# The last attention window's output product ahead of the expert tiles, and VectorE's routing cut into other pieces

## The reference

```
x: [2, 2048, 256], 16 heads of 16
scores  = 0 everywhere, q.k/4 inside each window of 128, plus q.k/4 among 64 global tokens
attn    = softmax(scores over all 2048 keys) @ v        # keys outside the window count with score 0
x1      = layernorm(x + attn @ wo.T + bo)
expert  = argmax(x1 @ Wg.T) over 8 experts
xhat    = layernorm(x1)
h       = gelu((xhat * ln_scale[e] + ln_bias[e]) @ W1[e] + b1[e])      # 64 wide
y       = h @ W2[e] + b2[e]                                            # e = expert of the token
out     = layernorm(x1 + y)
```

## Time and profile before

| what | us |
|---|---|
| runs of the kernel (3) | 398.56, 399.14, 401.33; median 399.14 |
| the profiled execution | 401.99 |
| its span, first to last instruction | 400.2 |
| busy in the span: PE, DVE, ACT, POOL | 342.2, 284.2, 226.9, 201.5 |

### The profile page before, as it was taken

How to read it: one execution, slowest core, us unless ns; L and a number is a source line. 1 busy time by engine, 2 the same in 40 slices (tenths; PEclk the granted TensorE clock), 3 DMA queues, 4 the chain that set the end, 5 groups by cost and what they waited for, 6 DMA issues and landing times.

```text
span 400.2 us, 12415 instructions
## 1 busy us (share of the span) xinstructions
PE 342.2 (85%) x4438; PEld 284.0 (71%) x4438; DVE 284.2 (71%) x829; ACT 226.9 (57%) x521; POOL 201.5 (50%) x352
## 2 busy tenths in 40 slices
PE   4989899999999999999989999988775798999400
PEld 3858688887887888887868888776453786877300
DVE  7795547676567675777888778796968796788810
ACT  3325476655665566556658866656653444777620
POOL 5243133443553435434447877844854343376772
PEclk9999999999999999999999999999999688999855
DMA  8762662100000000001013212100113554563220
GB/s 236 227 208 70 207 199 85 28 2 26 26 1 26 7 20 26 4 28 28 2 29 70 85 51 91 43 16 2 72 44 100 152 198 127 152 206 107 87 83 0
DMA packets 27981, 31.74 MB, mean 79 GB/s; under 512 B 5183, under 2 KB 25882, under 8 KB 27931
## 3 DMA queue, kind: packets, MB, share of 16 engines
q1 hardware_dynamic: 20246, 18.22, 15.9%
q0 software_dynamic: 3456, 8.66, 5.9%
q10 hardware_dynamic: 4230, 4.22, 3.2%
HBM read 20.96 MB, written 11.17 MB: 80 GB/s over the span
## 4 chain that ended last, share of the span: by engine, by line
PE 54%; DVE 24%; issue 7%; ACT 7%; POOL 3%; DMA 2%; SPq 0%; POOLq 0%; DVEq 0%; ACTq 0%
DVE row_max_t L1186 13%; PE ps L1436 8%; PE ps L1473 8%; PE ps L1398 7%; PE ps L1428 6%; PE ps L1703 5%; PE ps L1456 4%; PE ps L1721 3%; ACT probs L896 3%; PE ps L1450 3%; POOL out_dram L719 2%; PE ps L1420 2%; PE ps L1689 2%; PE ps L1440 2%; ACT boundsT_t L907 2%
## 5 line engine op out<-in xcount | busy, mean ns | idle before, releaser
L896 ACT ACTIVATE probs<-ps 128x1024 f32<-128x1024 f32 x64 | 62.1, 1022 | 59.9 <-PE ps L1440 59.7
L1186 DVE TENSOR_REDUCE row_max_t<-ps 128x16 f32<-128x2048 f32 x31 | 70.9, 2286 | 21.5 <-PE ps L1428 21.4
L1436 PE MATMUL ps<-q_slots,k_slots 32*128 32x256 f32 x512 | 40.5, 400 | 10.2 <-DVE row_max_t L1186 9.1
L663 POOL TENSOR_TENSOR attn_t<-num_t,rden_t 128x256 f32<-128x256 f32 x32 | 19.9, 621 | 54.1 <-DVE rden_t L1215 54.0
L746 ACT ACTIVATE pvT_t<-ps 128x512 f32<-128x512 f32 x34 | 20.3, 598 | 38.6 <-PE ps L1450 35.8
L646 POOL TENSOR_TENSOR bounds_t<-guard_t,bounds_t 128x16 f32<-128x16 f32 x32 | 7.1, 222 | 68.8 <-DVE guard_t L1197 68.7
L1428 PE MATMUL ps<-k_slots,q_slots 32*128 32x128 f32 x1056 | 38.7, 283 | 3.0 <-DVE dg L1037 1.3
L1428 PEld LDWEIGHTS ps<-k_slots,q_slots 32*128 32x128 f32 x1056 | 32.5, 186 | 8.9 <-issue 6.0
L719 POOL DMA_INDIRECT out_dram<-other_tiles x32 | 31.5, 985 | 11.7 <-issue 7.0
L907 ACT ACTIVATE boundsT_t<-ps,head_mask 128x128 fp32r<-128x128 f32 x128 | 36.7, 381 | 0.9 <-PE ps L1619 0.7
L620 POOL DMA_INDIRECT sorted_rows<-rows,place_i x32 | 31.7, 990 | 10.1 <-issue 6.3
(11 more groups left out here) (278 smaller groups left out, 796.9 us busy)
## 6 DMA issues: line engine op xcount, KB each, us to landing
table<-rest_sums SPq DMA_DIRECT2D x4, 1088.0 KB, 6.1
other_tiles<-sorted_rows SPq DMA_DIRECT2D x32, 136.0 KB, 2.4
xs<-in_L_attn_x_dram SPq DMA_DIRECT2D x16, 256.0 KB, 2.7
rows<-in_L_attn_x_dram ACTq DMA_DIRECT2D x4, 1024.0 KB, 7.4
sorted_rows<-pad_rows SPq DMA_DIRECT2D x9, 136.0 KB, 1.8
first_tiles<-sorted_rows SPq DMA_DIRECT2D x8, 136.0 KB, 2.1
w<-in_L_ffn_W_dram SPq DMA_DIRECT2D x2, 256.0 KB, 8.2
w<-in_L_ffn_W_dram SPq DMA_DIRECT2D x1, 512.0 KB
```

What stands on the lines that cost most here:

```text
L896: act.activation(probs[:, 2 * h:2 * h + 2, :], ps[:, 2 * h:2 * h + 2, :], ACT.Exp).then_inc(probs_ready, 1)
L1186: dve.tensor_reduce(row_max[:], ps_all, op=ALU.max, axis=AX.X).then_inc(max_ready, 1)
L1436: mm(ps[:, u, 2 * c * P:(2 * c + 2) * P], k_slots[quad(u), s, c, :], q_slots[quad(u), s, c, :, :].rearrange("p a n -> p (a n)"), start=Tru ...
```

## The change

It sets `PAIRS_FROM` to 34, so pair 0 comes at the end of step 34, behind the output product of window 31; pair 1 follows the ranks of the last batch in step 35. `turn_tiles(0)` and the registers of pair 0 move to the end of step 33. In `pair_steps` the registers of pair i+1 are read behind the first layer of pair i, except at pair 8, where the second list begins.

`route` is cut in two: `choose` takes its last three operations and, for the first batch, runs within step 19. The ranks of that batch come in step 20, its places in step 20, its factors in four pieces in steps 21 to 23. ACT's scalings start in step 24 and POOL's scatters in step 25, the last ones of the first two batches in step 31. The scalings of the third batch move from step 35 to 34, those of the fourth from pair 3 to pair 2.

The groups of results become seven: (0,2), (2,4), (4,8), (8,12), (12,16), (16,18), (18,20) in pairs. `list_tiles(1)` comes after `finish(1)` and the first `normalise` in place of after `finish(0)`.

```diff
--- before.py
+++ after.py
@@ -449,12 +449,12 @@
         LOOP_A = (4, 16)
         AHEAD = 2
         WEIGHTS_AT = 22
-        RANKS_AT = (19, 27, 33, 35)
-        PAIRS_FROM = NW + 1
-        SCALED_AT = {22: (0, 5), 23: (5, 10), 24: (10, 16), 29: (16, 20), 30: (20, 24), 35: (24, 30)}
-        SCATTERED_AT = {23: (0, 2, 3), 24: (3, 5, 6), 25: (6, 8, 9), 26: (9, 11, 12), 27: (12, 14, 15), 28: (15, 16, 16),
-                        30: (16, 19, 20), 31: (20, 22, 23), 32: (23, 24, 24)}
-        FACTORS_DONE = {22: 1, 29: 2, 35: 3}
+        RANKS_AT = (20, 27, 33, 35)
+        PAIRS_FROM = NW + 2
+        SCALED_AT = {24: (0, 5), 25: (5, 10), 26: (10, 16), 29: (16, 20), 30: (20, 24), 34: (24, 30)}
+        SCATTERED_AT = {25: (0, 2, 3), 26: (3, 5, 6), 27: (6, 8, 9), 28: (9, 11, 12), 29: (12, 14, 15), 30: (15, 18, 19),
+                        31: (19, 22, 24)}
+        FACTORS_DONE = {24: 1, 29: 2, 34: 3}
 
         def attention_steps(eng, step, first, split=None, between=None):
             for t in range(first, LOOP_A[0]):
@@ -473,7 +473,7 @@
 
 
 
-        GROUPS = ((0, 2), (2, 6), (6, 10), (10, 14), (14, 18), (18, 20))
+        GROUPS = ((0, 2), (2, 4), (4, 8), (8, 12), (12, 16), (16, 18), (18, 20))
 
         def final_places():
 
@@ -840,7 +840,7 @@
                     keep_tiles(i + 1)
                 for g, t in FINALS[i]:
                     final(g, t)
-                if i == 3:
+                if i == 2:
                     act.wait_ge(ln_ready, NB)
                     act.wait_ge(centred, NW)
                     for w in range(*BATCHES[-1]):
@@ -863,8 +863,10 @@
                 if not steady and t == 3:
                     act.wait_ge(out_gate_in_psum, 1)
                     copy(out_biasT[:].rearrange("p c n -> p (c n)"), ps_rao[:, HID:2 * HID]).then_inc(out_biasT_ready, 1)
-                if not steady and t > PAIRS_FROM:
-                    pair_steps(t - PAIRS_FROM - 1)
+                if not steady and t == PAIRS_FROM:
+                    keep_tiles(0)
+                if not steady and t >= PAIRS_FROM:
+                    pair_steps(t - PAIRS_FROM)
                 if not steady and t == 0:
                     act.wait_ge(xsum_in_psum, 1)
                     copy(pvT[:], ps_rao).then_inc(xsum_ready, 1)
@@ -881,8 +883,6 @@
                     act.activation(e_val[:, 1 - p, :], e_arg[:, 1 - p, :], ACT.Exp).then_inc(e_ready, 1)
                 if live(t + 1, steady) and p:
                     values_of(t + 1, (s + 1) % SLOTS, False)
-                if not steady and t == PAIRS_FROM:
-                    keep_tiles(0)
                 if not steady and t in SCALED_AT:
                     if t in FACTORS_DONE:
                         act.wait_ge(ln_ready, FACTORS_DONE[t])
@@ -912,7 +912,7 @@
 
             attention_steps(act, step, first=0)
 
-            for i in range(NW + 3 - PAIRS_FROM, PAIRS):
+            for i in range(NW + 4 - PAIRS_FROM, PAIRS):
                 pair_steps(i)
             keep_hidden(PAIRS - 1)
             for g, t in LAST_FINALS:
@@ -1099,6 +1099,13 @@
                 link(dve.tensor_tensor(zc[:, part, :], z_all[:, part, :], gate_bias[:].unsqueeze(1).broadcast_to(per_expert), ALU.add))
                 link(dve.tensor_reduce(zmax[:, 0, part], zc[:, part, :], op=ALU.max, axis=AX.X))
                 link(dve.tensor_tensor(hit[:, part, :], zc[:, part, :], zmax[:, 0, part].unsqueeze(2).broadcast_to(per_expert), ALU.is_equal))
+
+            def choose(b):
+
+                first, end = BATCHES[b]
+                n = end - first
+                part = slice(first, end)
+                per_expert = [P, n, EXPERTS]
                 link(dve.tensor_tensor(hit[:, part, :], hit[:, part, :], rank[:].unsqueeze(1).broadcast_to(per_expert), ALU.mult))
                 link(dve.tensor_reduce(zmax[:, 1, part], hit[:, part, :], op=ALU.max, axis=AX.X))
                 dve.tensor_tensor(onehot[:, part, :], hit[:, part, :], zmax[:, 1, part].unsqueeze(2).broadcast_to(per_expert),
@@ -1249,12 +1256,14 @@
 
                 if t == 17:
                     late_constants()
+                if t == 19:
+                    choose(0)
                 if t == 21:
-                    factors(0, 9, FACTOR_STEPS)
+                    factors(0, 0, 4)
                 if t == 23:
+                    factors(0, 10, FACTOR_STEPS)
+                if t == 25:
                     select_parts()
-                if t == 25:
-                    hidden_constants()
                 if t == 28:
                     factors(1, 4, 8)
                 if t == 30:
@@ -1263,16 +1272,21 @@
 
             def between_steps(t):
 
+                if t == 16:
+                    hidden_constants()
                 if t == 18:
                     route(0)
-                if t == 19:
+                if t == 20:
                     find_places(0)
-                if t == 20:
-                    factors(0, 0, 9)
-                if t in (21, 22):
-                    scale_first_layer(t - 21)
+                if t == 21:
+                    factors(0, 4, 6)
+                if t == 22:
+                    factors(0, 6, 10)
+                if t in (24, 25):
+                    scale_first_layer(t - 24)
                 if t == 26:
                     route(1)
+                    choose(1)
                 if t == 27:
                     find_places(1)
                     factors(1, 0, 4)
@@ -1286,6 +1300,7 @@
                     fold_first_bias()
                 if t == 32:
                     route(2)
+                    choose(2)
                     mark_tiles(0)
                     stack_first_bias()
                 if t == 33:
@@ -1293,6 +1308,7 @@
                     factors(2, 0, FACTOR_STEPS)
                 if t == 34:
                     route(3)
+                    choose(3)
                 if t == 35:
                     take_ranks(3)
                     dve.wait_ge(ranks_taken, NB)
@@ -1381,11 +1397,11 @@
             attention_steps(dve, step, first=0)
             for i in range(PAIRS):
                 finish(i)
-                if i == 0:
-                    list_tiles(1)
                 for g, (a, b) in enumerate(GROUPS):
                     if b == i + 1:
                         normalise(g)
+                if i == 1:
+                    list_tiles(1)
 
 
         @block.tensor
@@ -1552,8 +1568,6 @@
                     pe.wait_ge(v_ready, t - 1)
                     pe.wait_ge(boundsT_ready, upto(t))
                     weigh(va[:, (s + 2) % SLOTS, 0:HEADS * VP], probs).then_inc(pv_in_psum, 1)
-                if not steady and t == PAIRS_FROM:
-                    turn_tiles(0)
                 if not steady and t == 0:
                     sum_windows()
                 if not steady and t == 0:
@@ -1636,6 +1650,10 @@
                 if not steady and t == RANKS_AT[-1]:
                     pe.wait_ge(residual_ready, NW)
                     ranks(NB - 1)
+                if not steady and t == PAIRS_FROM - 1:
+                    turn_tiles(0)
+                    pe.wait_ge(lists_ready, 1)
+                    held[0] = experts_of(0)
                 if not steady and t >= PAIRS_FROM:
                     pair_steps(t - PAIRS_FROM)
 
@@ -1727,10 +1745,12 @@
                 if i == 0:
                     pe.wait_ge(experts_ready, 1)
                     pe.wait_ge(ld_w2, 32)
-                if 2 * i in (0, TILES[0]):
-                    pe.wait_ge(lists_ready, 1 + (i > 0))
-                held[i] = experts_of(i)
+                if 2 * i == TILES[0]:
+                    pe.wait_ge(lists_ready, 2)
+                    held[i] = experts_of(i)
                 first_layer(i, held[i])
+                if i + 1 < PAIRS and 2 * (i + 1) != TILES[0]:
+                    held[i + 1] = experts_of(i + 1)
                 if i > 0:
                     turn_hidden(i - 1)
                 if i + 1 < PAIRS:
```

## The result

The changed kernel is slower: median 410.25 us (410.14 to 410.98, 4 runs) against 399.98 (398.56 to 401.33, 4 runs of the kernel before). The ratio is 1.0261, with a 95% interval of 1.0218 to 1.0304, so about 10 us. 395.0 was forecast, in a range of 392.0 to 398.9.

What follows compares the result with a forecast made beforehand. DVE's reduction in the attention steps, PE's idle and low-clock seam, and POOL's scatters at the end were taken to bound the kernel. -1.8 - 1.2 - 0.6 + 0 - 0.4 = -4.0 off 399.14 gave 395.0 us, range 392.0 to 398.9.

Steps and rivals of the forecast that it cites:

- the registers read ahead in the steady pairs: Steady pairs on PE: reading the next pair's registers behind a first layer costs 0 us, bounds +0.8 and -1.0.
- 308.3 + 1.4: Seam: window 31's output product starts at about 309.7 us, once pair 0's registers are read behind the transposes.
- Attention steps: Steps 19 to 31: moved routing pieces, scalings and scatters gain 1.8 us, between 0.8 and 2.8.
- four factor pieces: Behind step 22: four of DVE's factor pieces outlast their 1.95 us of cover, -0.4 us of gain, bounds 0 and -1.0.
- 0.3 forecast: Attention steps: moving ACT's five scalings out of step 23 gains 0.3 us.
- Seam and second load: Seam: the second load frees PE at 333.7 or 336.3 us against 336.70; -1.2 us, between -3.0 and -0.4.
- Pair 3 was to start at 320.3 or 322.9: Seam: pair 3 starts at 320.3 us if PE's clock is full for pair 2, else 322.9, in old trace times.
- The reason given for PE's wait ahead of pair 2: Seam: ACT scales the third batch ahead of Gelu of pair 1, so PE waits about 1 to 1.7 us.
- Low clock after the second load: Behind the second load: PE's second clock fall, half of 1.4 us saved; -0.6 us, bounds 0 and -1.4.
- The list behind the first `normalise`: Seam: the second list ends at 329.0 or 331.5 us, old trace times, replacing the scatter as last before the load.
- The rival with 402: Seam: the later list costs more than it gave, and low clock costs two pairs more; 402 us, chance 0.06.
- Groups: End of kernel: POOL's last run has 16 scatters left in place of 20; -0.4 us, bounds -0.9 and 0.

Runs made afterwards that it cites:

- e2: Kernel before, with only the registers of pair i+1 read behind the first layer of pair i: 410.90 us, ratio 1.0228.
- e1: Changed kernel, but each pair above 0 reads its own registers ahead of its own first layer again: 402.28 us, ratio 1.0020.
- e5: Kernel before, with only the routing cut and moved, and scalings and scatters of the first two batches: 397.94 us, ratio 0.9932.
- e8: Kernel before, with only the new order of the seam; list, groups and later pairs' register reads as before: 401.26 us, ratio 1.0023.
- e3: Changed kernel, with the next pair's two registers read at the end of a pair, behind the second layer: 401.01 us, ratio 0.9996.
- e12: Changed kernel, reads at the pair's end, second list back behind `finish(0)`, third batch scaled in step 35 as before: 400.19 us, ratio 0.9997.
- e6: Changed kernel, with reads at the pair's end and the second list back behind `finish(0)`: 399.05 us, ratio 0.9944.
- e7: Kernel before, with seven groups of results in place of six and nothing else: 400.56 us, ratio 0.9990.
- e10: Kernel before, with the routing changes alone plus the next pair's registers read at the end of a pair: 397.02 us, ratio 0.9907.
- e9: Changed kernel, with two more, unused register reads behind the first layer, four in all: 439.58 us, ratio 1.0974.

## Why the prediction was wrong

**The step that failed** is "the registers read ahead in the steady pairs: before, no idle time of size shows there, so 0, bounds +0.8 (the read now stands between a first layer and the turn behind it) and -1.0". The place was named rightly, 0.8 us too; but it stood as the worst of the whole sum, and it is the price of each of 14 pairs. e2 measures +2.28%, 9.1 us on 401.3; taking the reads back out of the changed kernel (e1) says 9.7, from 1.0261 to 1.0020. The 0 rested on an absence: no idle time in the steady pairs says that two reads are hidden behind a pair's end, where the turned tiles (0.60 us) and the second layer (1.03) are still to run. It doesn't say that they are free anywhere else. The price lay in the earlier trace rows: two reads in the open leave PE idle for 1.35 and 1.40 us, 0.7 each, and the prediction used it in the same paragraphs ("308.3 + 1.4"). Two reads at 0.7 behind a first layer leave 0.8 if only some 0.6 us of matmuls cover them, four then leave 2.2 and one 0.1: measured 0.8, 1.8 to 2.45, and 0 to 0.54. That PE's sequencer handles reads and matmuls in one order, and runs ahead of the array only by that cover, is argued from these numbers. What would have warned: PE sets the end in the late pairs, as the prediction says itself, so each thing put between two of its instructions counts once for every pair.

**Attention steps**, -1.8 between -0.8 and -2.8: right. From the reduction of step 16 to that of step 31 the trace gives -1.76 (127.37 against 129.13), e5's -1.54, and e5 2.7 us in the whole time. By pieces: step 19 got its 0.80 back (0.82 forecast), 20 got 0.56 (0.56), 21 1.06 (1.19 before the factors). The four factor pieces made the step into 23 0.55 longer than the 8.20 of a plain one (0.4 forecast), and the step into 24 is back at 7.91 without ACT's scalings (0.3 forecast). The rule of the Trainium skill ("SBUF — State Buffer", "Who interferes with whom") was weighed there: a DVE instruction with two SBUF inputs contends with a GpSimd instruction that reads SBUF. The trace agrees in part, with 0.28 for the multiply moved into the step (0.62 before, where POOL worked without a break) and 0.94 for the factor piece left at the end of one. But not every such operation is stretched: just ahead of that multiply the compare of the kernel before, with two SBUF inputs too, took 0.29 at 183.47, while POOL was at work from 182.93 to 183.59.

**Seam and second load**, -1.2 between -3.0 and -0.4: the order came as described (DVE at 309.90, a wait for ACT's copy ahead of pair 2, the list as last in place of the scatter), the gain didn't. Alone it is +0.23% with an interval that holds 0 (e8). Pair 3 was to start at 320.3 or 322.9, less the 1.8 of the steps; it started at 322.03, later than both, with pair 2 at the lower level. The new order goes with a lower mean clock over many runs (0.949 against 0.956 in e8); that the new waits for `onehot` and for ACT cause it isn't shown, and e3's trace speaks against the second. The reason given for PE's wait ahead of pair 2, ACT's scalings, doesn't hold in the changed kernel's trace nor in e12. The step took a gain of DVE's for one of PE's: the last ranks were moved between pair 0 and pair 1, where PE waits 1.53 for DVE.

**Low clock after the second load**, -0.6 between 0 and -1.4: this second fall does go (PEclk 1.00 after 330 in e8), but the first one lasts longer. They were counted apart; in e8 it is a shift from one to the other.

**The list behind the first `normalise`**: it became last, as foreseen; the queue of SP waits 4.9 us for it in the changed kernel and 2.6 in e3, and not at all before. It was over at 330.95, where the forecast less the 1.8 of the steps says 327.2 to 329.7: pair 2 and the second layers that `finish(1)` waits for ran at the lower level. In e3's trace, at full clock, it was over at 327.70. The rival with 402 needed a list that costs more than it gives; e3 against e6 says about 2 us, less than that, and in the changed kernel itself PE never waits for the load, since its pairs are slow.

**Groups**, -0.4: right in number (16 scatters from the start of the last run), and not measurable (e7).

**The sum by what the runs showed:** reads +9.1, routing -2.7, seam order +0.9, groups -0.4 (these two not clear of 0) make +6.9. The list's 2 us would make it +8.9, but they were measured where PE gets to the load early; in the changed kernel it doesn't wait for it. Measured are 10.3, with an interval of 8.7 to 12.2, so up to 3.4 us stay without a cause that a run shows. The intervals of the parts, 1.2 to 1.8 us to either side of each, could hold that much. Every rival of the prediction turned on the seam or the steps; none was about the reads ahead, so the range had no room for this result, though it named the place.

## What to carry to other kernels

An instruction that shows no idle time is hidden by what is queued ahead of it; before moving it, find its bare price where it stands uncovered in the same trace, compare it with the cover at the new place, and multiply by the times it runs. Prefetching an iteration ahead doesn't help if it is issued where the engine's own queue is short: behind a long run of queued work it is hidden, but gained nothing measurable here over reading at once (e3, e10). A part of a mixed change is worth measuring by itself: here one part cost 9 us and hid that another gained 2.7.

## What the runs showed of the hardware

By estimate a register read on PE's queue costs about 0.7 us where nothing covers it (1.35 and 1.40 us for two in the earlier trace rows, and 1.0 to 1.65 more hole for four than for two). The profile has no record of the read; it puts the hole down to the last semaphore event near it, ACT's, and to "issue" once the hole is long enough.

Runs of one kernel differ by more than most parts of this change, along with the mean granted clock: runs of the kernel before with 0.946 took 401.5 to 403.5 us, with 0.968 398.2 to 398.5. The traces show where: the same order of the seam ran from 310 to 320 at a mean of 0.62 in one execution and 0.92 in another. Holes of about 0.8 us in every pair didn't make the clock fall: PEclk is 1.00 from 330 to 345 in the changed kernel, with PE busy for 11.67 of 15 us. Holes of over 2 us in e9 went with a mean of 0.916.
